# Spreading the hats of a deformable convolution in four 32-row groups of TensorE

## The reference

```python
wi = conv(x, w_offset) + b_offset            # 27 numbers per position: 9 dy, 9 dx, 9 masks
py = o1 + base_y;  px = o2 + base_x          # where each of the 9 taps looks
dy = py - floor(py);  dx = px - floor(px)
sampled = (v00*(1-dy)*(1-dx) + v01*(1-dy)*dx + v10*dy*(1-dx) + v11*dy*dx) * mask
out = einsum('bkcp,fck->bfp', col, w)        # project the 9 taps
```

## Time and profile before

| | |
|---|---|
| time, median of three runs | 402.97 us |
| span of the profiled execution, first to last instruction | 400.1 us |
| what lies around the span | about 2.9 us (402.97 less 400.1) |
| PE busy over the span | 315.2 us, 79% |
| DVE, ACT, POOL busy | 227.3, 195.6, 228.9 us |
| first projection of the first and of the last band | 51.88 and 241.71 us |

### The profile page before, as it was taken

One profiled execution on the slowest core, in us unless ns is written; L12 is line 12 of the kernel. 1 busy time (PEld: TensorE's weight loads), 2 busy tenths in 40 slices (PEclk: granted clock), 3 DMA queues, 4 the chain that ended last, 5 costly groups with the idle time before them and its releaser, 6 DMA issues.

```text
span 400.1 us, 9901 instructions
## 1 busy us (share of the span) xinstructions
PE 315.2 (79%) x2395; PEld 264.9 (66%) x2395; DVE 227.3 (57%) x988; ACT 195.6 (49%) x526; POOL 228.9 (57%) x351
## 2 busy tenths in 40 slices
PE   0999799999999999999999995049989797885000
PEld 0354688888889888898898994038867686774000
DVE  3983257878778787787887876502222122332085
ACT  1253566565565665756656652314444444442063
POOL 4013043777777777777777766204777777777300
PEclk9999899999999999999999999558999999999555
DMA  8958612222222222222222220855777777762298
GB/s 209 274 164 249 265 54 75 89 80 100 78 93 85 82 99 78 90 94 76 98 84 83 95 80 26 145 139 169 223 222 243 230 231 232 227 221 72 82 315 234
DMA packets 52450, 57.88 MB, mean 145 GB/s; under 512 B 6892, under 2 KB 40423, under 8 KB 52424
## 3 DMA queue, kind: packets, MB, share of 16 engines
q1 hardware_dynamic: 45031, 48.16, 39.1%
q0 software_dynamic: 4544, 8.44, 6.6%
q10 hardware_dynamic: 2848, 0.99, 1.4%
HBM read 30.70 MB, written 14.97 MB: 114 GB/s over the span
## 4 chain that ended last, share of the span: by engine, by line
PE 53%; SPq 16%; issue 10%; DMA 6%; ACT 4%; DVE 4%; POOL 2%; ACTq 2%; DVEq 1%; POOLq 0%
PE bank L1326 18%; PE bank L1315 15%; SPq L481 5%; PE bank L1248 5%; SPq L490 4%; SPq L496 3%; DMA wide<-result 2%; PE bank L1279 2%; PE bank L1433 2%; ACT samp L758 2%; PE bank L1269 2%; PE bank L1260 2%; POOL result L658 2%; DMA routed<-padding_sb 1%; DMA result<-y,to 1%
## 5 line engine op out<-in xcount | busy, mean ns | idle before, releaser
L658 POOL DMA_INDIRECT result<-y,to x78 | 76.8, 985 | 43.8 <-DVE to L1191 26.8
L1326 PE MATMUL bank<-filt_sb,samp 128*128 128x128 f32 x576 | 79.3, 283 | 4.1 <-ACT samp L758 2.5
L1326 PEld LDWEIGHTS bank<-filt_sb,samp 128*128 128x128 f32 x576 | 69.1, 191 | 18.1 <-ACT samp L758 14.2
L1315 PE MATMUL bank<-S,xwin 100*128 100x144 f32 x512 | 78.9, 298 | 1.8 <-issue 1.7
L602 POOL DMA_INDIRECT routed<-payload,slot x64 | 63.2, 987 | 18.5 <-issue 13.5
L758 ACT ACTIVATE samp<-bank 128x432 f32<-128x432 f32 (+1 forms) x96 | 46.3, 484 | 52.8 <-PE bank L1315 52.8
L1315 PEld LDWEIGHTS bank<-S,xwin 100*128 100x128 f32 x512 | 67.7, 193 | 2.2 <-issue 2.0
L923 DVE TENSOR_TENSOR S<-ysp,bank 100x512 f32<-100x512 f32 (+1 forms) x96 | 52.5, 550 | 22.9 <-ACT ysp L729 21.8
L1433 PE MATMUL bank<-rowsT,w_blk 128*128 128x256 f32 x156 | 44.4, 408 | 13.3 <-DMA w_blk<-w_all 10.2
L1199 DVE TENSOR_TENSOR y<-bank,w_blk 128x256 f32<-128x256 f32 x39 | 16.6, 425 | 66.0 <-PE bank L1442 64.2
L822 ACT ACTIVATE rowsT<-bank 128x256 f32<-128x256 f32 x39 | 15.0, 384 | 61.0 <-PE bank L1424 61.0
(11 more groups left out here) (110 smaller groups left out, 493.1 us busy)
## 6 DMA issues: line engine op xcount, KB each, us to landing
w_blk<-w_all SPq DMA_DIRECT2D x39, 321.0 KB
xwin<-lines SPq DMA_DIRECT2D x64, 120.0 KB
xwin<-lines SPq DMA_DIRECT2D x32, 160.0 KB
rows_in<-routed SPq DMA_DIRECT2D x39, 129.0 KB
wide<-result SPq DMA_DIRECT2D x16, 256.0 KB, 4.8
w_all<-in_experts SPq DMA_DIRECT2D x4, 642.0 KB, 7.4
out_tiles<-res SPq DMA_DIRECT2D x8, 256.0 KB, 4.6
wide<-in_x_rows SPq DMA_DIRECT2D x3, 512.0 KB, 8.6
```

Of the source, the lines that this page charges most:

```text
L658: nc.gpsimd.indirect_dma_start(result, bass.IndirectOffsetOnAxis(to[:, slot, j:j + 1].bitcast(U32), 0), y[:, slot, j, :], None, bounds_che ...
L1315: last = nc.tensor.matmul(bank[5 + (par + g) % 2][:, i * TAPS * TT:(i + 1) * TAPS * TT], xwin[:, par, t, :], weights[:, t], start=True, st ...
L1326: last = nc.tensor.matmul(bank[7][:, 0:C], samp[:, par, j, :], filt_sb[:, order[j], :], start=(j == 0), stop=(j == TAPS - 1))
```

## The change

A row of `hat3` gets 2 x 32 numbers per tap: 30 of y (three parts of ten) and two zeros, then 30 of x and two zeros. Two transposed taps fill 128 rows, in four groups of 32 that start at rows 0 (even y), 32 (even x), 64 (odd y) and 96 (odd x). A spread matmul takes only the 30 rows of its own group, and `spread_sb` shrinks to one block of 100 columns. In the built program such a matmul carries the tile size 32 rows x 128 columns with the row position 0, 32, 64 or 96, where it carried 128 x 128. The matmuls of u = 0 and u = 1 stand together where u = 0 stood, ahead of `count_places`; u = 2 stays where it was, between the two parts of `project`. The waits of both groups are carried by one instruction ahead of them (`settle`), so that y of u = 2 now waits for `S_ready` as x did.

```diff
-SLOT = PARTS * HATS
+GROUP = 32
+SLOT = 2 * GROUP
...
-        hat3 = sb("hat3", [P, 2, TAPS + 1, SLOT], BF16)
+        hat3 = sb("hat3", [P, 2, TAPS + 1, 2, GROUP], BF16)
...
-            nc.gpsimd.memset(hat3[:, :, TAPS, :], 0.0).then_inc(s.zeroed, 1)
+            nc.gpsimd.memset(hat3[:, :, :, :, :], 0.0).then_inc(s.zeroed, 1)
...
-                h3 = hat3[:, par, 0:TAPS, :].rearrange("p k (part h) -> p part k h", part=PARTS)
-                h = hat[:, par, :].rearrange("p (k h) -> p k h", k=TAPS)
+                hi, mid, lo = (hat3[:, par, 0:TAPS, :, part * WIN:(part + 1) * WIN] for part in range(PARTS))
+                h = hat[:, par, :].rearrange("p (k yx j) -> p k yx j", k=TAPS, yx=2)
...
-            def spread_hats(b, par, u):
-                pe.wait_ge(s.hatT_ready, b + 1)
-                slot, n, odd = (par + u) % 2, UNITS[u], u % 2
-                moving = hatT[:, 4, :] if u == 2 else hatT[:, 0:4, :].rearrange("r i t -> r (i t)")
-                at_least(pe, s.y_ready, b * 3 + u - 1)
-                nc.tensor.matmul(bank[slot][0:Q, 0:n], spread_sb[:, 2 * odd, :], moving,
-                                 start=True, stop=True).then_inc(s.y_psum, 1)
-                at_least(pe, s.S_ready, b * 3 + u - 1)
-                nc.tensor.matmul(bank[2 + slot][0:Q, 0:n], spread_sb[:, 2 * odd + 1, :], moving,
-                                 start=True, stop=True).then_inc(s.x_psum, 1)
+            def spread_taps(par, u):
+                slot, n, odd = (par + u) % 2, UNITS[u], u % 2
+                for yx, arrived in ((0, s.y_psum), (1, s.x_psum)):
+                    first = GROUP * (2 * odd + yx)
+                    rows = slice(first, first + PARTS * WIN)
+                    moving = hatT[rows, 4, :] if u == 2 else hatT[rows, 0:4, :].rearrange("r i t -> r (i t)")
+                    nc.tensor.matmul(bank[2 * yx + slot][0:Q, 0:n], spread_sb[rows, :], moving,
+                                     start=True, stop=True).then_inc(arrived, 1)
+            def spread_hats(b, par):
+                pe.wait_ge(s.hatT_ready, b + 1)
+                at_least(pe, s.y_ready, b * 3)
+                at_least(pe, s.S_ready, b * 3)
+                settle(pe)
+                spread_taps(par, 0)
+                spread_taps(par, 1)
+            def spread_last(b, par):
+                pe.wait_ge(s.y_ready, b * 3 + 1)
+                pe.wait_ge(s.S_ready, b * 3 + 1)
+                settle(pe)
+                spread_taps(par, 2)
...
-                        spread_hats(b, par, 0)
+                        spread_hats(b, par)
...
-                        spread_hats(b, par, 1)
...
-                        spread_hats(b, par, 2)
+                        spread_last(b, par)
```

More of the change, by code:

```diff
@@ L104, in window_constants @@
     rel[:, :, 1, :] += (dx[:, None] + kx[None, :] + HALO)[:, :, None] - j
-    spread = np.zeros((2, PARTS, 2, WIN, 2, 2, Q), np.float32)
+    spread = np.zeros((2, 2, GROUP, Q), np.float32)
     q = np.arange(Q)
[L108 to L112, removed]
+    for part in range(PARTS):
+        spread[:, 0, part * WIN + q % WIN, q] = 1
+        spread[:, 1, part * WIN + q // WIN, q] = 1
+    spread = spread.reshape(2 * SLOT, Q)
     fold = np.zeros((4, 32, OFFS), np.float32)
@@ L163, in program @@
         rel_sb = sb("rel_sb", [P, TAPS * HATS])
-        spread_f = sb("spread_f", [2 * SLOT, 4, Q])
-        spread_sb = sb("spread_sb", [2 * SLOT, 4, Q], BF16)
+        spread_f = sb("spread_f", [2 * SLOT, Q])
+        spread_sb = sb("spread_sb", [2 * SLOT, Q], BF16)
         fold_sb = sb("fold_sb", [P, OFFS])
@@ L385, in load_consts @@
                 load(rel_sb[:, :], rel)
-                load(spread_f[:, :, :], spread.rearrange("r (f q) -> r f q", f=4))
+                load(spread_f[:, :], spread)
                 load(before_f[:, :], before)
@@ L560, in _ @@
             pool.wait_ge(s.consts_loaded, 16 * N_CONSTS)
-            nc.gpsimd.tensor_copy(spread_sb[:, :, :], spread_f[:, :, :]).then_inc(s.tables_ready, 1)
+            nc.gpsimd.tensor_copy(spread_sb[:, :], spread_f[:, :]).then_inc(s.tables_ready, 1)
             nc.gpsimd.tensor_copy(identb_sb[:, :], ident_sb[:, :]).then_inc(s.tables_ready, 1)
@@ L573, in split @@
             def split(b, par):
-                h3 = hat3[:, par, 0:TAPS, :].rearrange("p k (part h) -> p part k h", part=PARTS)
-                h = hat[:, par, :].rearrange("p (k h) -> p k h", k=TAPS)
-                r = rest[:, par, :].rearrange("p (k h) -> p k h", k=TAPS)
+                hi, mid, lo = (hat3[:, par, 0:TAPS, :, part * WIN:(part + 1) * WIN] for part in range(PARTS))
+                h = hat[:, par, :].rearrange("p (k yx j) -> p k yx j", k=TAPS, yx=2)
+                r = rest[:, par, :].rearrange("p (k yx j) -> p k yx j", k=TAPS, yx=2)
                 pool.wait_ge(s.hi_ready, b + 1)
-                nc.gpsimd.tensor_tensor(r, h, h3[:, 0], ALU.subtract).then_inc(s.pool_step, 1)
-                nc.gpsimd.tensor_tensor(h3[:, 1], h, h3[:, 0], ALU.subtract).then_inc(s.pool_step, 1)
+                nc.gpsimd.tensor_tensor(r, h, hi, ALU.subtract).then_inc(s.pool_step, 1)
+                nc.gpsimd.tensor_tensor(mid, h, hi, ALU.subtract).then_inc(s.pool_step, 1)
                 pool.wait_ge(s.pool_step, b * 2 + 2)
-                nc.gpsimd.tensor_tensor(h3[:, 2], r, h3[:, 1], ALU.subtract).then_inc(s.hat3_ready, 1)
+                nc.gpsimd.tensor_tensor(lo, r, mid, ALU.subtract).then_inc(s.hat3_ready, 1)
             def pack(b, par):
@@ L714, in hi_part @@
                 act.wait_ge(s.hat_ready, b + 1)
-                nc.scalar.activation(hat3[:, par, 0:TAPS, 0:HATS],
-                                     hat[:, par, :].rearrange("p (k h) -> p k h", k=TAPS),
+                nc.scalar.activation(hat3[:, par, 0:TAPS, :, 0:WIN],
+                                     hat[:, par, :].rearrange("p (k yx j) -> p k yx j", k=TAPS, yx=2),
                                      ACT.Copy).then_inc(s.hi_ready, 1)
@@ L1269, in transpose_hats @@
                     last = nc.tensor.transpose(bank4b[0:2 * SLOT, i * P:(i + 1) * P],
-                                               hat3[:, par, 2 * i:2 * i + 2, :].rearrange("p k r -> p (k r)"),
+                                               hat3[:, par, 2 * i:2 * i + 2, :, :].rearrange("p k yx r -> p (k yx r)"),
                                                identb_sb[:, :])
                 last.then_inc(s.hatT_psum, 1)
-            def spread_hats(b, par, u):
-                pe.wait_ge(s.hatT_ready, b + 1)
-                slot, n, odd = (par + u) % 2, UNITS[u], u % 2
-                moving = hatT[:, 4, :] if u == 2 else hatT[:, 0:4, :].rearrange("r i t -> r (i t)")
-                at_least(pe, s.y_ready, b * 3 + u - 1)
-                nc.tensor.matmul(bank[slot][0:Q, 0:n], spread_sb[:, 2 * odd, :], moving,
-                                 start=True, stop=True).then_inc(s.y_psum, 1)
-                at_least(pe, s.S_ready, b * 3 + u - 1)
-                nc.tensor.matmul(bank[2 + slot][0:Q, 0:n], spread_sb[:, 2 * odd + 1, :], moving,
-                                 start=True, stop=True).then_inc(s.x_psum, 1)
+            def spread_taps(par, u):
[7 more added lines that the diff above has]
+            def spread_hats(b, par):
+                pe.wait_ge(s.hatT_ready, b + 1)
+                at_least(pe, s.y_ready, b * 3)
[8 more added lines that the diff above has]
+                spread_taps(par, 2)
             transpose_image(0)
@@ L1295, in _ @@
                 fold_groups(m, 1)
-            for u in range(3):
-                spread_hats(0, 0, u)
+            spread_hats(0, 0)
+            spread_last(0, 0)
             pe.wait_ge(s.near_ready, 3 * IMAGES)
```

## The result

The kernel after takes 413.35 us, the median of 4 runs (412.03 to 414.10), beside 402.99 (402.83 to 403.05) of the kernel before on the same chip: a ratio of 1.0258, 95% interval 1.0238 to 1.0278. Forecast were 409.5 us and a range of 402.4 to 412.3. The sign was right, the size was not: +10.4 us instead of +6.5, and just above the range.

A forecast was written before the change was run, and what follows sets the result against it. It took a 6.18 us loop over PE, DVE and ACT to bound the kernel; 31 bands x 0.21 us gave +6.5, all other terms 0, so 400.1 + 6.5 = 406.6, plus 2.9 around the span: 409.5 us, range 402.4 to 412.3.

The forecast's parts named there:

- What bounds the kernel: Band loop of 6.18 us: projection with u = 2 on PE, residual on DVE, root and copies on ACT.
- The four large spreads, gain 0: The 512-column spreads on PE lie where it waits for ACT anyway; shortening them only adds idle time.
- u = 2: -0.06 + 0.13 + 0.14 = +0.21: Two small spreads on PE inside the loop: side by side, entering and leaving row groups; +0.21 us a band, bounds +0.12 to +0.40.
- entering: PE's change from 128 rows to 32-row groups ahead of u = 2: +0.13 us, bounds 0.09 and 0.20.
- leaving: PE's change back from row groups to 128 rows behind u = 2: +0.14 us, bounds 0.09 and 0.20.
- The rest, 0: Shorter runs in POOL's `split` and ACT's `hi_part`, larger transposes and copy: 0, at most 0.02 us a band for `hi_part`.
- The range: Forecast of the total time: 402.4 to 412.3 us, upper end at 0.30 us a band; the bounds reached 415.4.
- The start, 0: Ahead of the bands: larger clearing of `hat3` while the first matmul waits for DVE, smaller table loaded behind the images: 0.
- Free: Rival at u = 2: row groups cost nothing to enter and leave, -1.9 us, 401.1 us; chance 0.16.
- cancelled: Rival at u = 2: each mode change costs about 0.03 us, paid for by the pair's 0.06; 403.0 us; chance 0.10.
- not side by side: Rival for all spreads on PE: groups run one after another, 0.37 us a band, 414.4 us; chance 0.05.

The follow-up runs named there:

- e1: Kernel after with only the two u = 2 spreads put back on all 128 rows, tables padded with zeros: 403.32 us, ratio 0.9994 to the kernel before.
- e3: Kernel before with four extra 128-column spreads a band at u = 2, ahead of the last taps, no row groups: 412.16 us, ratio 1.0229.
- e9: Kernel after with POOL's small copy of pack moved ahead of the two scatters, so the second scatter starts later: 411.10 us, ratio 1.0153.
- e2: Kernel after with only the four large spreads put back on all 128 rows, one behind the other: 414.93 us, ratio 1.0275.
- e4: Kernel after with POOL's scatter of the band three back issued ahead of the distances of the band three on: 455.59 us, ratio 1.1272.
- e6: e1 with two moves: ACT's second copy of samples ahead of the root, DVE's place row ahead of normalise: 401.22 us, ratio 0.9945.
- e8: Kernel before with two moves: ACT's second copy of samples ahead of the root, DVE's place row ahead of normalise: 399.22 us, ratio 0.9880.
- e10: e7 with the two u = 2 spreads parted by two taps, so PE enters and leaves the row groups twice a band: 418.63 us, ratio 1.0346.
- e7: Kernel after with two moves: ACT's second copy of samples ahead of the root, DVE's place row ahead of normalise: 405.34 us, ratio 1.0038.
- e12: Kernel before with eight extra 128-column spreads a band at u = 2, ahead of the last taps, no row groups: 413.68 us, ratio 1.0225.
- e5: Kernel after with L908 alone rewritten as an operation with two input tensors, the second a tile of zeros: 411.63 us, ratio 1.0197.

## Why the prediction was right in sign and wrong in size

- *What bounds the kernel.* Right. The loop over projection, residual, root and copies decided the kernel after, e1, e3 and e9, and the four spreads outside of it moved nothing in e1. Other paths came up only where an experiment made them late: DVE's places in e2, POOL's distances in e4.
- *The four large spreads, gain 0.* Right, measured by e1 against the kernel before and by the loops of e6 and e8. The wait for ACT rose to 0.57 us (about 0.6 predicted).
- *u = 2: -0.06 + 0.13 + 0.14 = +0.21.* The sum is right (+0.22; e9: period 6.39, +6.2 us), its parts less so, and that is some luck. In the means of the bands the first spread starts 0.20 us behind the token transpose instead of 0.11 (entering +0.09, forecast 0.13). The second starts 0.003 behind the first instead of 0.06 (-0.06, as forecast). The first tap starts 0.18 behind that instead of 0.06, and the next tap 0.21 behind the first instead of 0.16 (leaving +0.18, forecast 0.14). Two misses of 0.04 cancel. By the Trainium skill, TensorEngine Tiling (Array Packing), section Tiling Modes under Key Properties, a change of mode drains the engine; e10 agrees for row groups, with 0.20 us in and 0.18 out, twice.
- *The rest, 0.* This step failed, and with it the sentence that a delay in the loop reaches the next projection in full, as if in full were also the most. What I costed there held: `hi_part` takes 0.34 us before and after, `split`'s step 0.53 and 0.52. But the loop's leg on DVE, from L931 to L939, went into the sum as unchanged, at 0, without a look at what an unchanged instruction meets when it moves 0.22 us against another engine. L908 slid from 0.21 to 0.47 us into POOL's scatter and was held to its end: +0.15 us a band net, 9.7 - 31 x 0.22 = 2.9 us over the loop, of the 3.9 that were missing. Of the rest 0.3 are the 0.22 against 0.21 a band, and 0.7 lie outside the loop, open. Shown by e3 (a delay of the same size does it without row groups), e9 (a later scatter undoes it) and e7 (out of the loop it costs nothing); e12 shows that a delay can also cost less than its length, 0.30 a band for 0.45.
- *The range.* The bounds reached to 415.4; I cut the forecast's own at 412.3 because the rows showed no gap to be a whole loss. The trace gave no reason to cut there.
- *The start, 0.* The bands begin at 54.51 us in the profile of the kernel after and at 51.88 before, but e4, with the start of the kernel after, begins them at 51.77 and e8, with that of the kernel before, at 53.47. These 2.6 us belong to the execution, not to the change. So does the size of what lies around the span: it is 1.8 to 2.1 us in every execution that has both numbers, not 2.9, so that by my estimate the profiled execution before took about 402 us. The sum ends at the median plus 6.5 all the same and is not touched by it.
- *The rivals.* Free, cancelled and not side by side all fell: PE shows 0.39 us about the pair, and the four large ones take 0.42 us together.

## What to carry to other kernels

A faster operation that needs another mode of an engine can pay for the way in and out: count the crossings on the path, not the matmuls saved. Here one more way in and out cost 0.37 us (e10), while the two plain matmuls that the pair replaced had taken 0.12. When a delay goes into a loop, don't stop at its own length: list what each engine does at that moment against a clock that does not move with it, and ask what the shifted instructions will meet. If two engines collide, look at the order of work on either: e9's one copy gave back 1 of the 2.6%. And once the loop is known, a move of order on it can do what the change did not: e8's two moves made the kernel before 1.2% faster.

## What the runs showed of the hardware

L908, a DVE instruction from SBUF to SBUF, runs freely beside POOL's scatter or is held to the scatter's end, and its start all but tells which. In seven traces (before, after, e1, e3, e6, e8, e9) none of 102 L908 that started up to 0.285 us behind the second scatter's start was long. Of 74 that started 0.287 to 0.573 us behind it 69 were, with their ends 0.05 us behind the scatter's; of the other five, four stand in the last two bands of a run and one, at 0.290, in the loop of e8. e5's form with two inputs and, in e10, L904 are held too.

The scatter's end is no fixed mark either. Over all runs but e5, and without the last two bands, a held L908 that starts 0.29 to 0.50 us into the scatter takes 0.70 us wherever it starts, and the scatter grows: 0.96 us for a start before 0.34, 1.01 around 0.36, 1.09 around 0.44 and 1.12 around 0.47. At 0.57 L908 takes 0.44 and the scatter 0.96 again. Why is not shown.

By the Trainium skill, SBUF — State Buffer, section SBUF: two separate sides, whichever of a DVE operation in a mode with two ports and a GpSimd operation starts first holds the shared ports for the whole instruction. Here the wait agrees; that it begins only some 0.3 us into the scatter (0.25 us for L908 at 209.53, inside a scatter from 209.32 to 210.29) does not. Whether L908 runs in such a mode no run shows.
